# Moving the subtract and multiply of two layer norms from VectorE to GpSimd, in a fused convolution, attention and mixture-of-experts kernel

## The reference, cut to what matters

```python
x = x + conv_attention(group_norm(x))     # 4 heads, 256 keys; its output goes through a layer norm over 128 (ln_g, ln_b), then a 128x128 matrix
t = to_tokens(x)                          # (4, 1024, 128)
t = t + attention(layer_norm(t))          # one head of 64, 1024 keys; attention() itself adds its normed input and a bias b_o
t = t + moe(layer_norm(t))                # router, 2 of 8 experts, hidden 341, silu
```

## Time and profile before

| | |
|---|---|
| device time, median of 3 runs | 539.91 us (537.53 to 542.23) |
| profiled execution, span from first to last instruction | 536.8 us, 11801 instructions |
| profiled execution, whole | not given beside the span |
| TensorE busy / VectorE / ScalarE / GpSimd | 463.2 / 339.2 / 297.3 / 182.4 us |
| mean granted TensorE clock over the span | 0.959 |

### The profile page before, as it was taken

How to read it: one execution, slowest core, us unless ns; L and a number is a source line. 1 busy time by engine, 2 the same in 40 slices (tenths; PEclk the granted TensorE clock), 3 DMA queues, 4 the chain that set the end, 5 groups by cost and what they waited for, 6 DMA issues and landing times.

```text
span 536.8 us, 11801 instructions
## 1 busy us (share of the span) xinstructions
PE 463.2 (86%) x3494; PEld 364.5 (68%) x3495; DVE 339.2 (63%) x1015; ACT 297.3 (55%) x782; POOL 182.4 (34%) x199
## 2 busy tenths in 40 slices
PE   3848899878789998989999988898979989999981
PEld 3537677666567777677787776587857767877761
DVE  4643496598764679686876977855764444435652
ACT  1227777678855777866666655345424433443440
POOL 4001001033131041010485372477657753343340
PEclk9959999889979999999999999999989999999995
DMA  8588540802001703011041011122222431227524
GB/s 260 135 203 236 180 106 21 227 1 60 22 0 55 194 1 79 2 41 40 2 119 41 17 51 51 41 71 76 71 55 69 108 94 49 56 54 213 155 95 142
DMA packets 40059, 46.88 MB, mean 87 GB/s; under 512 B 6523, under 2 KB 29524, under 8 KB 40004
## 3 DMA queue, kind: packets, MB, share of 16 engines
q1 hardware_dynamic: 34234, 36.07, 25.6%
q0 software_dynamic: 4608, 9.99, 5.5%
q10 hardware_dynamic: 1162, 0.14, 0.2%
HBM read 24.66 MB, written 17.85 MB: 79 GB/s over the span
## 4 chain that ended last, share of the span: by engine, by line
PE 56%; DVE 17%; issue 10%; ACT 8%; DMA 6%; ACTq 1%; SPq 1%; POOL 1%; DVEq 0%; POOLq 0%
PE S L1434 12%; PE PO L1450 8%; PE S L1271 7%; PE TA L1442 3%; PE OM L1291 3%; ACT shared L711 3%; DVE lowest L902 3%; PE S L1257 3%; PE S L1258 2%; PE TA L1367 2%; DVE shared L911 2%; DMA xs<-slots 2%; PE OM L1285 1%; PE S L1253 1%; ACT shared L727 1%
## 5 line engine op out<-in xcount | busy, mean ns | idle before, releaser
L902 DVE TENSOR_REDUCE lowest<-S 128x4 f32<-128x1024 f32 (+1 forms) x64 | 78.0, 1219 | 56.5 <-PE S L1253 29.4
L1434 PE MATMUL S<-w_T,shared 128*128 x284 | 95.1, 457 | 3.9 <-ACT shared L809 3.0
L621 POOL DMA_INDIRECT y_rows<-shared,xs x71 | 68.3, 962 | 78.9 <-ACT shared L820 69.6
L1271 PE MATMUL S<-ident,shared 128*128 128x128 f32 x512 | 74.4, 286 | 6.4 <-ACT shared L711 4.0
L727 ACT ACTIVATE shared<-S 128x512 f32<-128x512 f32 (+1 forms) x64 | 51.9, 811 | 49.7 <-PE S L1271 49.6
L1183 DVE TENSOR_TENSOR late<-S,shared 128x341 f32<-128x341 f32 x71 | 36.4, 513 | 63.7 <-ACT shared L814 63.3
L814 ACT ACTIVATE shared<-S 128x341 f32<-128x341 f32 x71 | 32.4, 456 | 78.7 <-PE S L1434 77.6
L615 POOL DMA_INDIRECT slots<-rows_both,pos_i x64 | 62.4, 974 | 30.6 <-issue 17.8
L1271 PEld LDWEIGHTS S<-ident,shared 128*128 128x128 f32 x512 | 59.9, 146 | 16.7 <-ACT shared L711 9.1
L1450 PEld LDWEIGHTS PO<-w_T,shared 114*128 114x128 f32 x426 | 53.6, 193 | 23.4 <-issue 16.4
L1450 PE MATMUL PO<-w_T,shared 114*128 x426 | 61.4, 281 | 9.0 <-DVE shared L1188 5.6
(11 more groups left out here) (287 smaller groups left out, 814.7 us busy)
## 6 DMA issues: line engine op xcount, KB each, us to landing
CQ<-q_pass SPq DMA_DIRECT2D x24, 256.0 KB, 5.3
xs<-slots SPq DMA_DIRECT2D x71, 65.0 KB, 1.9
CQ<-CQ SPq DMA_DIRECT2D x16, 256.0 KB, 2.9
late<-y_rows SPq DMA_DIRECT2D x8, 512.0 KB, 4.8
q_pass<-late SPq DMA_DIRECT2D x6, 512.0 KB, 3.5
x<-in_x SPq DMA_DIRECT2D x4, 512.0 KB, 5.5
out<-x SPq DMA_DIRECT2D x8, 256.0 KB, 2.2
CK<-k_pass SPq DMA_DIRECT2D x12, 128.0 KB, 3.3
```

What stands on the lines that cost most here:

```text
L621: pool.indirect_dma_start(y_rows, bass.IndirectOffsetOnAxis(xs[:, k, C:C + 1].bitcast(I32), 0), ys[:, k % NC, :], None).then_inc(ys_out[k] ...
L902: nc.vector.tensor_reduce(lowest[:, g % 2, 0:n], S[g % 2][:, :].rearrange("p (h k) -> p h k", h=n), AX.X, ALU.min).then_inc(s["low_ready"], 1)
L1271: last = tr(S[g % 2][:, tile(k)], probs[:, g % 2, tile(k)], ident[:, :])
L1434: last = mm(S[k % 2][:, m * 512:m * 512 + H], xsT[:, k % NC, :], w13_T[:, bass.ds(e, 1), m * H:(m + 1) * H].rearrange("p a h -> p (a h)"), ...
```

## The change

The subtract and multiply of the first two layer norms (ca0, ca1, ta0, ta1) are issued on GpSimd, in the same slots, behind the power that GpSimd computes itself. Those of the third (pa0, pa1: rows to be sent) stay on VectorE and signal a semaphore of their own, `sent_ready`. VectorE's statistics now wait, ahead of L951 which overwrites `mv`, until GpSimd is through with all earlier applies.

```diff
+        def applied_before(f):
+            return 2 * sum(g[0] in ("cs1", "ts1") for g in NORMS[:norm_of(f)])
+        def sent_before(f):
+            return 2 * sum(g[0] == "ps1" for g in NORMS[:norm_of(f)])
...
 # GpSimd
+            def apply_norm(f, src, half):
+                wait_if(pool, s["fill_done"], banked_before(f))
+                wait_if(pool, s["tok_ready"], 2 * before_it(f, "ta1"))
+                pool.wait_ge(s["norm_rstd"], norm_of(f) + 1)
+                for i in range(4 * half, 4 * half + 4):
+                    last = nc.gpsimd.tensor_scalar(normed_of(f)[:, i, :], src[:, i, :], mv[:, i, 0:1], rs_y[:, i:i + 1],
+                                                   ALU.subtract, ALU.mult)
+                last.then_inc(s["normed_ready"], 1)
             def fill(u, b):
                 f = (u, b)
+                if u in ("ca0", "ca1"):
+                    apply_norm(f, conv_out[b % 2], int(u[-1]))
+                elif u in ("ta0", "ta1"):
+                    apply_norm(f, tok[b], int(u[-1]))
                 if f in NORMS:
...
-                    pool.wait_ge(s["normed_ready"], 2 * norm_of(f) + 2)
+                    pool.wait_ge(s["normed_ready"], applied_before(f) + 2)
...
 # ScalarE, unit pc
-                    act.wait_ge(s["normed_ready"], 2 * norm_of(f) + 2)
+                    act.wait_ge(s["sent_ready"], sent_before(f) + 2)
...
 # VectorE, statistics
                 link(last)
+                wait_if(dve, s["normed_ready"], applied_before(f))
                 for i in tiles:
...
 # VectorE, apply_norm
-                wait_if(dve, s["tok_ready"], 2 * before_it(f, "ta1"))
-                if f[0][0] == "p":
-                    dve.wait_ge(s["init_z"], 4)
-                    wait_if(dve, s[f"dispatched{f[1] % 2}"], 16 * 2 * NT * (f[1] // 2))
+                dve.wait_ge(s["init_z"], 4)
+                wait_if(dve, s[f"dispatched{f[1] % 2}"], 16 * 2 * NT * (f[1] // 2))
...
-                last.then_inc(s["normed_ready"], 1)
+                last.then_inc(s["sent_ready"], 1)
...
-                elif u in ("ca0", "ca1"):
-                    apply_norm(f, conv_out[b % 2], half)
...
-                elif u in ("ta0", "ta1"):
-                    apply_norm(f, tok[b], half)
...
 # TensorE
-                    pe.wait_ge(s["normed_ready"], 2 * norm_of(f) + 1 + half)
+                    if u[0] == "r":
+                        pe.wait_ge(s["sent_ready"], sent_before(f) + 1 + half)
+                    else:
+                        pe.wait_ge(s["normed_ready"], applied_before(f) + 1 + half)
```

More of the change, by code:

```diff
@@ L275, in build @@
             pv_done ot_copied post_done post_used dve_step fill_done fill_copied0 fill_copied1 xn_ready
-            taps_ready hi_done norm_stats norm_step norm_rstd normed_ready tok_ready rows_set
+            taps_ready hi_done norm_stats norm_step norm_rstd normed_ready sent_ready tok_ready rows_set
             r_exp_in r_exp r_cnt_in route_done table index_set pad_in init_z init_done dispatched0 dispatched1 xs_in0
@@ L955, in apply_norm @@
             def apply_norm(f, src, half):
-                n = norm_of(f)
-                dve.wait_ge(s["norm_rstd"], n + 1)
+                dve.wait_ge(s["norm_rstd"], norm_of(f) + 1)
                 wait_if(dve, s["fill_done"], banked_before(f))
-                wait_if(dve, s["tok_ready"], 2 * before_it(f, "ta1"))
-                if f[0][0] == "p":
-                    dve.wait_ge(s["init_z"], 4)
-                    wait_if(dve, s[f"dispatched{f[1] % 2}"], 16 * 2 * NT * (f[1] // 2))
+                dve.wait_ge(s["init_z"], 4)
+                wait_if(dve, s[f"dispatched{f[1] % 2}"], 16 * 2 * NT * (f[1] // 2))
                 for i in range(4 * half, 4 * half + 4):
```

## The result

The change made the kernel slower: 544.32 us median of 20 runs against 539.23 of 20 runs of the kernel before, a ratio of 1.0105 (95% interval 1.0082 to 1.0127). By the ratio that is 5.7 us (0.0105 of 539.2), by the medians 5.1, where I had forecast 0.3. The 544.32 lies above the upper end of my range, 543.8. The profiled execution's span went from 536.8 to 543.8 us, 7.0 us; by its own run time, 545.58 us, it lies 1.3 us above the median of its 20 runs, so the pair shows more than the medians do.

What follows compares the result with a forecast made beforehand. TensorE, busy 86% and 56% of the chain, was read as leading, VectorE not the bound as a whole. Terms -0.16 - 0.18 + 1.36 - 0.75 = +0.27 us on the 539.9 median gave 540.2 us, range 536.6 to 543.8.

Steps and rivals of the forecast that it cites:

- the price of the moved instruction: One 128-column subtract-and-multiply on GpSimd was taken at 0.50 us, between bounds of 0.29 and 0.59.
- rival (b): Slower GpSimd makes TensorE wait in conv 2 and tok 1; about +7 us at 0.9 us an instruction, 547; chance 0.08.
- conv 2, c0(1) and c1(1): Image 1's transposes in conv 2: GpSimd's norm would be ready when TensorE comes, a gain of 0.18 us.
- turning point of 0.54 us: In conv 2, the price per instruction above which eight of them outlast c1(1)'s start at 135.43.
- tok 0, adds against the group norm: Start of tok 0: L985 would meet GpSimd's second add and be blocked to its end, 1.36 us lost.
- rival (a): At the tok 0 lock, a longer TensorE wait also costs clock; with conv 2, up to 3.5 us, 543.4; chance 0.15.
- tok 1: With ta0(3) off VectorE, the row minimum comes sooner and ScalarE's wait before the exponentials shrinks, a gain of 0.75 us.
- limit of 0.63 us for l1(3): In tok 1, the price per instruction up to which l1(3) would not wait for ta1(3) on GpSimd.
- conv 1: At c1(0), TensorE's idle 0.16 us for VectorE's ca1 would go, a gain for any price up to 1.2 us.
- the statistics' new wait, the queues and tok 0's ca(2): Waits ahead of L951, GpSimd's queued adds and dispatch, and ca(2) in tok 0 were priced at nothing.
- rival c: VectorE's relief counts in full, 4.0 us of L965 and 2.0 us of waiting on the chain: 533.9; chance 0.06.

Runs made afterwards that it cites:

- e5: The change with its moved instructions in seven forms to price them, single execution; a 128-column copy took 0.29 us, the change's own form 0.80.
- e10: The change with each moved instruction on only 64 of its 128 columns; ratio 0.9966 to the kernel before, 0.58 us an instruction.
- e1: The change with only the tokens' norm (ta0, ta1) on GpSimd, ca0 and ca1 back on VectorE; ratio 1.0129 to the kernel before.
- e3: The change with image 1's convolution norm, ca0(1) and ca1(1), back on VectorE; ratio 1.0034 to the kernel before.
- e11: The kernel before with only image 1's tokens' norm, ta0(1) and ta1(1), on GpSimd; ratio 1.0045 to the kernel before.
- e4: The change with GpSimd's two adds of image 1 waiting until the group norm of image 3 is done; ratio 1.0058 to the kernel before.
- e8: The kernel before, nothing moved, with the adds of image 1 behind the group norm of image 3; ratio 1.0008 to the kernel before.
- e13: The kernel before with only ta0(3) on GpSimd; ratio 1.0013 to the kernel before, span 534.0 us.
- e2: The change with only the convolution's norm (ca0, ca1) on GpSimd, ta0 and ta1 back on VectorE; ratio 1.0077 to the kernel before.
- e7: The change with ca0(1), ca0(3), ta1(3) back on VectorE and image 1's adds behind image 3's group norm; ratio 0.9974 to the kernel before.

## Why the prediction was wrong

**The step that failed is the price of the moved instruction.** I put it at 0.50 us with an upper bound of 0.59; it measured 0.79 (0.78 from start to start). My sum of +0.3 us became +5.7 through the terms below, and all three go back to this price. The bound was no bound. The line came from two one-operation instructions with a constant, and I had written under rival (b) that no two-operation instruction with per-partition operands was in the trace, without letting that widen the bounds of the price. e5 gives what was missing: 0.8 us against 0.53 for the form I had extrapolated.

**conv 2, c0(1) and c1(1): forecast -0.18, measured +3.93.** The mechanism is that of rival (b). The turning point of 0.54 us was near but somewhat high: at 0.56 (e10) TensorE waits 0.7 us and the stretch is 0.55 longer, at 0.78 it waits 2.5 in two places. What the clock adds, 1.6 us, I had priced there only in the rival.

**tok 0, adds against the group norm: forecast +1.36, measured +2.39.** The place, the two instructions and the lock were right. The size came from another alignment: at 0.78 us L1005 meets the first add just begun, not the second. I had followed the term only up to 0.59 us, where it drops; the first add brings it back, 147.8 + 6.2 = 154.0 for its start before L985's 154.64, and an end 0.56 us past the add's makes 156.9 in place of 155.8, 1.1 us; measured it is 1.24, 2.40 in place of 1.16. The rest, 1.15, goes with the longer stretch at half speed, rival (a)'s second part. That this term had the right sign is in part luck, then: at 0.50 us the group norm was to meet the second add, at 0.79 it met the first, and by my own working it would have met neither just above 0.55. The group norm took 2.40, 2.45, 2.53 and 2.48 us where it was issued 0.4 to 0.5 us behind the start of an add (after, e1, e3, e11) and 0.80 where no add ran (e4, e8) or the add was in its last 0.2 us (e10). The Trainium skill ("SBUF — State Buffer", "Who interferes with whom") has the two engines exclude each other there; the traces agree.

**tok 1: forecast -0.75, measured +1.31.** The gain exists, 0.59 alone (e13), but c1(3) costs 0.58 with the whole convolution norm moved (e2), and moving the tokens' norm costs 0.77 net (e1), since l1(3) waits 1.12 us; 0.58 + 0.77 comes to 1.35. My limit of 0.63 us for l1(3) and rival (b)'s times for c1(3) pointed at the same places.

**conv 1: forecast -0.16, measured -0.09.** TensorE's wait of 0.16 at c1(0) is gone, and the slack held at 0.79 us. A stretch of 0.1 us can't be told from nothing, where low clocks move it by 1.7. What the prediction left out is l1(0), at the start of conv 2: it had no term, and TensorE waits 1.3 us there where no low clock in conv 1 has made it late (e4, e7).

**The rest.** That the statistics' new wait, the queues and tok 0's ca(2) cost nothing was right, as far as the profiled pair shows: the stretches without those three places stay within 0.17 us. That VectorE's 4.0 us on the chain would not come back as such (rival c) was right too: 64 instructions off VectorE bought 0.6 us. Rival (b), with its 0.08, was the case, below the 0.9 us that it was worked out for. Its +7 us and the +7.0 of the profiled pair agree by luck: the rival had no lock in its sum, and of the 7.0 the group norm's stretch has 2.4.

## What to carry to other kernels

Price an instruction that no row shows by its own form: operand kinds and the number of operations belong to it, and where they are missing the bound is open upwards. Then ask of each moved instruction when its reader comes and what is queued behind it: here the mean load of both engines said nothing, three places of 1.3 to 3.9 us held all of the loss, and one of them was two adds that nobody was waiting for. Compare stretches between like instructions, since one execution's span moves by more than such an effect.

## What the runs showed of the hardware that I had not expected

On GpSimd a multiply of two tensors of 128 columns took 0.46 us, less than one TENSOR_SCALAR with a constant on the same size (0.53), and two TENSOR_TENSORs over 512 columns with a broadcast operand took 2.1 us where four TENSOR_SCALARs took 3.1. And TensorE's half speed behind waits of about 1.8 us was there in some executions of the same instructions and not in others, which moves a span by 1 to 2 us at each place. Three such places, one of them with a shorter wait as well, made 4.5 us in e13. What decides it these runs don't show.
